# Gated cross-attention and quantised feed-forward: the mask becomes the bias of seven exponentials, scores move to PSUM, and the attention loop is put in another order

## The reference

```python
def _L0_xattn_ref(q, kv_src, seg_id, Wq, Wkv, Wo):
    qh = _split_heads(q @ Wq.T)
    k, v = jnp.split(kv_src @ Wkv.T, 2, axis=-1)
    gather = seg_id[:, :, None] - jnp.arange(4)
    neg_mask = gather < 0
    gc = jnp.clip(gather, 0, lkv - 1)
    k_sel, v_sel = kh[b_idx, :, gc], vh[b_idx, :, gc]       # transposed to b h q k d
    scores = jnp.einsum('bhqd,bhqkd->bhqk', qh, k_sel) * SCALE
    scores = jnp.where(neg_mask[:, None], neg_inf, scores)
    out = jnp.einsum('bhqk,bhqkd->bhqd', jax.nn.softmax(scores, axis=-1), v_sel)
    return out.transpose(0, 2, 1, 3).reshape(b, lq, D_ATTN) @ Wo.T

x = x + tanh(g_xattn[0]) * _L0_xattn_ref(layernorm(x), ctx, seg, Wq, Wkv, Wo)
x = x + tanh(g_ffn[0]) * _L0_ffn_ref(layernorm(x), W_in, b_in, W_out, b_out)
```

## Time and profile before

| | us |
|---|---|
| median of 3 runs | 355.43 (355.17 to 357.68) |
| the profiled execution | 353.4, its span 351.6 |
| busy: TensorE / VectorE / ScalarE / GpSimd | 289.5 / 316.8 / 207.7 / 171.8 |
| setup until the first product | 22.4 |
| attention loop (products of steps 1 to 16) | 22.4 to about 206.5 |
| last steps of attention and setup of the feed-forward part | to 225.4 |
| feed-forward part | 225.4 to 351.6 |

### The profile page before, as it was taken

The page is one execution under the profiler, slowest core; times in us unless marked ns, Lnnn a source line. Parts: engine busy times, 40 slices in busy tenths (PEclk is TensorE's granted clock), DMA queues, the critical chain, the costliest instruction groups (busy, mean ns, idle before and its releaser), DMA issues.

```text
span 351.6 us, 5786 instructions
## 1 busy us (share of the span) xinstructions
PE 289.5 (82%) x1807; PEld 210.5 (60%) x1807; DVE 316.8 (90%) x614; ACT 207.7 (59%) x323; POOL 171.8 (49%) x160
## 2 busy tenths in 40 slices
PE   3873779767679999999999955699799949999994
PEld 3442557555557777777777734344344418888883
DVE  0988599999998999999999999779999879999993
ACT  2132341251605666555556635899699969999991
POOL 1100638849497989889989882012243500110000
PEclk9998588885969999999999999699999998999999
DMA  7993000000000000000000000011112100435545
GB/s 259 282 389 111 0 0 0 2 1 0 2 2 0 0 2 0 3 0 2 1 2 1 3 0 0 0 62 60 60 61 102 77 1 2 62 60 76 98 64 119
DMA packets 6979, 17.26 MB, mean 49 GB/s; under 512 B 1318, under 2 KB 3822, under 8 KB 6446
## 3 DMA queue, kind: packets, MB, share of 16 engines
q1 hardware_dynamic: 4447, 12.31, 9.8%
q0 software_dynamic: 1008, 3.67, 6.8%
q10 hardware_dynamic: 1503, 1.02, 1.2%
HBM read 9.13 MB, written 7.86 MB: 48 GB/s over the span
## 4 chain that ended last, share of the span: by engine, by line
DVE 51%; PE 35%; issue 4%; ACT 4%; DMA 2%; POOL 2%; DVEq 0%; ACTq 0%; POOLq 0%
PE bank L786 16%; PE bank L756 12%; DVE prod L863 10%; DVE s L869 8%; DVE s L875 4%; PE bank L593 4%; DVE bn L820 3%; DVE xres L917 2%; DMA wq_ld<-in_L_xattn_Wq_dram 2%; PE bank L613 2%; DVE hmax L1117 2%; DVE onehot L969 2%; DVE xmax L923 2%; DVE s L884 2%; DVE bn L830 2%
## 5 line engine op out<-in xcount | busy, mean ns | idle before, releaser
L593 PE MATMUL bank<-kvtab,onehot 80*128 80x256 f16 x512 | 73.2, 291 | 26.3 <-DVE prod L863 17.1
L593 PEld LDWEIGHTS bank<-kvtab,onehot 80*128 80x128 bf16 x512 | 49.8, 103 | 46.1 <-DVE prod L863 22.4
L298 POOL TENSOR_TENSOR vsel<-vsel,pr 128x1024 f32<-128x1024 f32 x31 | 59.9, 1932 | 25.9 <-ACT vsel L348 20.3
L485 ACT ACTIVATE hidden<-bank,bin__58,zscale 128x512 f32 x64 | 49.6, 777 | 7.4 <-PE bank L756 2.2
L756 PE MATMUL bank<-xhi,win 128*128 128x512 f16 x128 | 49.3, 385 | 1.9 <-DVE xlo L1112 1.9
L756 PE MATMUL bank<-xlo,win 128*128 128x512 f16 x128 | 49.1, 384 | 0.0
L1177 DVE SCALAR_TENSOR_TENSOR hlo<-hq,rel_wout,hhi 128x512 f16<-128x512 int16 x64 | 46.0, 752 | 0.0
L863 DVE TENSOR_TENSOR prod<-bank,q 128x1024 f32<-128x1024 f32 x32 | 39.0, 1218 | 5.4 <-PE bank L593 5.3
L348 ACT ACTIVATE xT<-bank 128x512 f32<-128x512 f32 x16 | 9.5, 597 | 55.5 <-PE bank L644 55.5
L348 ACT ACTIVATE vsel<-bank 128x1024 f32<-128x1024 f32 x31 | 31.6, 1018 | 17.1 <-PE bank L593 17.1
L301 POOL TENSOR_TENSOR vsel<-vsel 128x512 f32<-128x512 f32 x31 | 40.4, 1302 | 2.4
(11 more groups left out here) (133 smaller groups left out, 479.8 us busy)
## 6 DMA issues: line engine op xcount, KB each, us to landing
xres<-in_x_dram SPq DMA_DIRECT2D x4, 1024.0 KB, 17.7
out_dram<-xres SPq DMA_DIRECT2D x7, 512.0 KB, 2.6
out_dram<-y POOLq DMA_DIRECT2D x7, 512.0 KB, 5.3
win_ld<-in_L_ffn_W_in_dram SPq DMA_DIRECT2D x1, 1024.0 KB, 12.4
wout_ld<-in_L_ffn_W_out_dram SPq DMA_DIRECT2D x1, 1024.0 KB, 23.1
seg_i<-in_itok_BxS_dram SPq DMA_DIRECT2D x3, 320.0 KB, 13.9
wkv_ld<-in_L_xattn_Wkv_dram SPq DMA_DIRECT2D x1, 512.0 KB, 4.9
seg_i<-in_itok_BxS_dram ACTq DMA_DIRECT2D x1, 320.0 KB, 9.2
```

Of the source, the lines that this page charges most:

```text
L298: pool.tensor_tensor(v3, v3, pr[k][:, t].rearrange("p o h -> p (o h)").unsqueeze(2).broadcast_to([P, KW * H, HD]), ALU.mult).then_inc(s_pv, 1)
L485: act.activation(hidden[:, g, f, :], bank, ACT.Gelu, bias=bin_[:, f:f + 1], scale=zscale[:, f:f + 1]).then_inc(s_h, 1)
L593: mm = pe.matmul(dst[:, off * D:(off + 1) * D], onehot[:, off, bass.ds(tile * P, P)], kvtab[:, b, part, col:col + D], start=(part == 0), s ...
```

## The change

Tables get three more rows in front (83 rows): an index below zero now gathers a copy of row 0, and its score is put out by a bias of -1e30 inside the exponential, a column of `neg` per tile and offset. So `mask` goes, and one exponential over 128 columns becomes seven: one of 32 columns for offset 0 of both tiles, six of 16 columns. Scores and exponentials share one place in PSUM, `sc`, in the first half of bank67, from which `ps_o` has moved out: the attention result's transpose now shares `ps_t` with the two other transposes.

The first norm of batches 1 to 3 moves from VectorE to ScalarE, in half batches of four tiles: sums, negative means, sums of squared differences. The clamps of batches 1 to 3 move to GpSimd, variance plus epsilon of the second norm from GpSimd to VectorE. `vsel` has four buffers instead of two. Lags change: v gathers and copies 1, residual 4, `norm_bias` 5, `norm2` 5, transpose of the second norm 6. The tables of batches 2 and 3 are scaled one at a time. W_out's maximum is taken after steps 13 and 14, its levels after step 15.

```diff
-                dve.tensor_tensor(s3, s3, neg[:, bass.ds(2 * u, 2), :]...broadcast_to([P, 2 * KW, H]), ALU.add).then_inc(s_masked, 1)
+        sc = [bank67[:, k * 2 * KW * H:(k + 1) * 2 * KW * H].rearrange("p (t o h) -> p t o h", t=2, o=KW) for k in range(2)]
...
             def exp(u, k):
                 act.wait_ge(s_shift, u + 1)
-                act.activation(e[k][:].rearrange(...), s[k][:].rearrange(...), ACT.Exp, scale=SCALE).then_inc(s_exp, 1)
+                act.activation(sc[k][:, :, 0, :], sc[k][:, :, 0, :], ACT.Exp, scale=SCALE)
+                for t in range(2):
+                    for off in range(1, KW):
+                        ins = act.activation(sc[k][:, t, off, :], sc[k][:, t, off, :], ACT.Exp,
+                                             bias=neg[:, 2 * u + t, off:off + 1], scale=SCALE)
+                ins.then_inc(s_exp, 1)
...
+            def stats1(b, half):
+                n = 2 * (b - 1) + half
+                act.wait_ge(s_x[b], 16)
+                if n:
+                    act.wait_ge(s_ssq1, n)
+                at = slice(b * TB + half * (TB // 2), b * TB + (half + 1) * (TB // 2))
+                for t in range(at.start, at.stop):
+                    ins = act.activation(unread[0][:, t % (TB // 2), :], xres[:, t, :], ACT.Copy, accum_out=sum1[:, t:t + 1])
+                ins.then_inc(s_sum1, 1)
+                act.wait_ge(s_sum1, n + 1)
+                act.activation(nmean1[:, at], sum1[:, at], ACT.Copy, scale=-1.0 / D).then_inc(s_nmean1, 1)
+                act.wait_ge(s_nmean1, n + 1)
+                for t in range(at.start, at.stop):
+                    ins = act.activation(unread[1][:, t % (TB // 2), :], xres[:, t, :], ACT.Square, bias=nmean1[:, t:t + 1],
+                                         accum_out=ssq1[:, t:t + 1])
+                ins.then_inc(s_ssq1, 1)
...
+            def clamp_seg(b):
+                pool.wait_ge(s_segb[b], 16)
+                pool.tensor_scalar(seg_b[:, b * LQ:(b + 1) * LQ]..., seg_i[:, b * LQ:(b + 1) * LQ]...,
+                                   float(TOP), 0.0, ALU.min, ALU.max).then_inc(s_segc, 1)
...
-            act.dma_start(ctx_ld[LKV:U, :, :], ctx_kv[:, LKV - 1, :].partition_broadcast(U - LKV)).then_inc(s_ctx, 16)
+            act.dma_start(ctx_ld[LB + LKV:U, :, :], ctx_kv[:, LKV - 1, :].partition_broadcast(LB)).then_inc(s_ctx, 16)
+            act.dma_start(ctx_ld[0:LB, :, :], ctx_kv[:, 0, :].partition_broadcast(LB)).then_inc(s_ctx, 16)
...
# TensorE's step
+                if on(0):
+                    transpose_x(i, k)
+                if on(1):
+                    gather_k(i - 1, 0)
+                    gather_v(i - 1, 0)
+                if on(6):
+                    transpose_xn2(i - 6, k, (s_xT, i + 1) if on(0) else (s_oT, i - 3))
+                if on(0):
+                    queries(i, k)
+                if on(1):
+                    gather_k(i - 1, 1)
+                if on(3):
+                    transpose_o(i - 3, 1 - k, (s_xn2T, i - 5) if on(6) else (s_xT, i + 1))
+                if on(1):
+                    gather_v(i - 1, 1)
+                if on(3):
+                    attn_out(i - 3, 1 - k)
...
# VectorE: behind aggregate, and the order of its first steps
+                dve.wait_ge(s_mv, u + 1)
+                dve.tensor_scalar(ve[k][:], mv[k][:, :, 1], LN_EPS, None, ALU.add).then_inc(s_ve, 1)
...
+            kv_scales(2, 1)
+            step(1, 1, between=lambda: kv_low(2))
+            kv_scales(3, 1)
+            step(2, 0, between=lambda: kv_low(3))
+            make_onehot(1)
...
+            for i in range(3, NP + 1):
+                step(i, i % 2)
+                if i in (6, 10):
+                    make_onehot(i // 3)
+                if i in (NP - 3, NP - 2):
+                    wout_amax(i - NP + 3)
+                if i == NP - 1:
+                    wout_levels()
...
# ScalarE's loop
-            for i in range(2, NP + 2):
+            for i in range(2, NP + 1):
                 step(i, i % 2)
+                if i in (2, 4, 5, 7, 8):
+                    stats1((i + 2) // 3, 0 if i in (4, 7) else 1)
```

More of the change, by code:

```diff
@@ L579, in transpose_o @@
                     pe.wait_ge(s_olast, 1)
-                if first(u, 1):
-                    pe.wait_ge(s_oT, u)
+                pe.wait_ge(*free)
                 for t in range(2):
                     for c in range(C):
-                        mm = pe.transpose(ps_o[:, c * 2 * P + t * P:c * 2 * P + (t + 1) * P], o[k][:, t, c * P:(c + 1) * P], ident[:])
+                        mm = pe.transpose(ps_t[:, c * 2 * P + t * P:c * 2 * P + (t + 1) * P], o[k][:, t, c * P:(c + 1) * P], ident[:])
                 mm.then_inc(s_oTp, 1)
@@ L626, in transpose_xn2 @@
                     pe.wait_ge(s_xn2b, 1)
-                if isinstance(u, int) and u + 5 > NP:
-                    pe.wait_ge(s_xn2T, u)
-                else:
-                    pe.wait_ge(s_xT, u + 5)
+                pe.wait_ge(*free)
                 for t in range(2):
@@ L637, in transpose_x @@
                 pe.wait_ge(s_x[u // (TB // 2)], 16)
-                if first(u, 5):
-                    pe.wait_ge(s_xn2T, u - 4)
+                if u >= 4:
+                    pe.wait_ge(s_oT, u - 3)
                 elif u:
@@ L697, in _ @@
             pe.wait_ge(s_kvlo, 2)
-            gather_k(0, 0)
+            step(1, 1)
+            pe.wait_ge(s_kvlo, 3)
             project_kv(3)
-            step(1, 1)
             def spread(psum, ready, done):
@@ L1019, in _ @@
             for off in range(KW):
-                ins = dve.tensor_scalar(neg[:, :, off], seg_f[:], float(off), NEG, ALU.is_lt, ALU.mult)
+                ins = dve.tensor_scalar(neg[:, :, off], seg_f[:], float(off), NEG_BIAS, ALU.is_lt, ALU.mult)
             ins.then_inc(s_neg, 1)
             dve.wait_ge(s_neg, 1)
-            step(1, 1)
-            kv_scales(2)
+            kv_scales(2, 1)
[3 more added lines that the diff above has]
+            make_onehot(1)
+            dve.wait_ge(s_tanh, 1)
             def top_of(psum, ready, out):
@@ new lines, in _ @@
+            for i in range(3, NP + 1):
[6 more added lines that the diff above has]
+                    wout_levels()
+            norm_bias(NP - 4, 0)
+            softmax_end(NP - 1, 1)
+            residual(NP - 3, 1)
+            stats2(NP - 3, 1)
+            aggregate(NP - 3, 1)
+            weigh_last(NP - 1, 1)
```

294 lines of the change are left out of this document (140 added, 154 removed).

## The result

The changed kernel takes **396.35 us** (median of 4 runs, 394.91 to 397.13); the kernel before, on the same chip, 355.36. The ratio is 1.113 [1.108, 1.119]: 41 us slower where 17 us faster was forecast, and far above the range. The profiled execution has a span of 394.9 us against 351.6.

The account below looks back on a forecast made before the run. VectorE was taken to set the pace, with TensorE and GpSimd 3.6 and 4.0 us behind over five steps. Terms of +3.6, -10.2, -12.9, +0.8 and +1.5 sum to -17.2, giving 338 us against the median; range 329 to 350.

Parts of the forecast that it names:

- the start: Up to step 1's first product: one more DMA issue, one table's scales and GpSimd's clamps add 3.6 us.
- steps 1 and 2: First two attention steps: W_out's maximum, broadcast and gather wait leave; 29.4 us becomes 19.2, so -10.2.
- steps 3 to 10: Attention loop: VectorE loses three batches of first-norm statistics and two clamps; 96.7 us becomes 83.8, so -12.9.
- steps 11 to 16: Late attention steps: six of 9.2 us plus 3.6 for W_out's maximum, against 58.0 us before, so +0.8.
- the tail: Between loop and feed-forward part: one more group of residual, statistics and norm, plus W_out's ratio, adds 1.5 us.
- The plain step of 9.2: Attention loop: three rings between 8.8 and 9.1 us hand on lateness, giving 9.2 us a step against 9.67.
- the ring by way of `xT`: Two-step chain through ScalarE's exponentials and xT copy, TensorE's queries to gather, and VectorE's step: 18.1 us, 9.05 a step.
- the share of a half batch that comes through: Steps 3 to 10: of ScalarE's 3.3 us half batch, 1.7 to 2.0 us lengthens each of four full steps.
- The clamps at the start: Three clamps on GpSimd land on the first one-hot and stretch VectorE's work: +2.5 us, ends 0 and +5.
- The rival in which GpSimd holds variance plus epsilon: VectorE's new small operation waits for GpSimd, 0.7 us on average in 12 steps: +8.4, 346 us; chance 0.20.
- The slower rival: ScalarE becomes the bound: exponentials at 0.59 us each, steps of 10.5 us, half batches 5.2: 364 us; chance 0.08.
- TensorE's low clock: Rival: TensorE stays at the lower clock through steps 3 to 6 and becomes the bound: +8, 346 us; chance 0.12.

Follow-up runs that it names:

- e1: The changed kernel with the index loads broadcast to 96 partitions instead of 83, the other 13 rows never read: 362.14 us.
- e10: The changed kernel with each of its four index loads issued as two, to 80 rows and to the last 3: 361.42 us.
- e5_xt_first: e1 with ScalarE's copy of the transposed x (xT) put ahead of the seven exponentials instead of behind them: 349.89 us.
- e9: e5_xt_first with GpSimd's three clamps held until VectorE has written the mask table `neg`: 350.87 us.
- e13: e9 with ScalarE's tanh of the gates moved behind its step 1: 343.95 us, ratio 0.967.
- e6: e5_xt_first with GpSimd's three clamps held until the one-hot rows of batch 0 are done: 350.72 us.
- e14: e5_xt_first (clamps beside the one-hot rows) with ScalarE's tanh of the gates moved behind its step 1: 349.88 us.
- e3: The kernel before with the mask part alone: 83 clipped rows (loaded to 96), no mask, seven exponentials, scores in SBUF, old order: 363.87 us.

## Why the prediction was wrong

**The step that failed is the start**, "+3.6", and with it steps 1 and 2, "-10.2". ScalarE's one more DMA issue was counted, but the four index loads that change from 80 to 83 rows were taken to be the same. They were not looked at as transfers: the term had no row for them, and its ends (0 to +5, for the port) left them out. The runs put about 34 us on them (e1 against the changed kernel), and e10 shows that it is their shape and not their bytes. No rival had it.

Without that fault the forecast would still have been 26 us short. By the terms, e1 lies above it by 5.6 at the start, 4.1 in steps 1 and 2, 10.6 in steps 3 to 10, 0.7 in steps 11 to 16 and 5.4 in the tail.

**Steps 3 to 10**, "-12.9", failed as well: without the load fault they gave -2.3. From one step's product to the next's, in us (the one-hots of batches 2 and 3 fall into steps 6 and 10):

| step | 3 | 4 | 5 | 6 | 7 | 8 | 9 | 10 |
|---|---|---|---|---|---|---|---|---|
| forecast | 8.0 | 9.0 | 10.9 | 13.3 | 9.2 | 10.9 | 10.9 | 11.6 |
| e1_rows96 | 12.3 | 8.1 | 12.3 | 16.9 | 8.8 | 9.7 | 12.9 | 13.6 |
| e5_xt_first | 9.0 | 8.4 | 10.3 | 13.2 | 8.8 | 8.9 | 10.1 | 13.2 |

The plain step of 9.2, and with it the ring by way of `xT` at 9.05, was about right: 8.8 in step 7, 8.8 and 9.7 in steps 11 and 12. What failed is the share of a half batch that comes through, 1.7 to 2.0 us "in each of four full steps", reckoned from ScalarE's idle time. In e1, against 9.2, steps 3, 5, 6 (without its one-hots) and 9 are longer by 3.0 to 4.1 us, which is nearly the whole half batch; only in step 8 is it hidden but for 0.5. ScalarE's queue has exponentials and xT behind the half batch, and TensorE stands until xT is copied and then runs at a lower clock for a while. e5 moves only that copy, the half batches stay, and steps 3, 5, 6 and 9 give 11.7 of its 12.6 us. The price of the ring also left out the transpose of the second norm, 0.46 us, which stands between xT's copy and the queries; no run separates it.

The half batches themselves were mis-sized too: 3.95 us (72.34 to 76.29) instead of 3.3, since each sum brings a second instruction of 0.19 us that reads the accumulator. And the two groups of one-hots in e1 took 3.56 and 4.22 us where 2.4 was taken for each, 3.0 of the 10.6.

```profile
L467 ACT ACTIVATION_READ_ACCUMULATOR unread<-xres 128x1 f32 x24 | 4.6, 192 | 0.0
L473 ACT ACTIVATION_READ_ACCUMULATOR unread<-xres,nmean 128x1 f32 x24 | 4.5, 186 | 0.0
```

**The clamps at the start** cost more than their upper end of +5, where +2.5 was taken. The one-hots took 7.01 us beside three clamps with 96 rows, +5.1; beside one clamp, as the loads left it in the changed kernel, 3.61. Held back behind `neg` (e5 to e9), they let the first product start 7.1 us sooner. The gates' load has its row (3.5 us of waiting before `tanhs`), but the forecast didn't name it.

**The tail**, "+1.5", is +6.1 to +6.9 in three kernels. One more group of residual, statistics and norm was priced, but not that the last attention output waits its turn behind it on ScalarE. Exchanging the two gave nothing. What in the longer chain costs isn't separated.

**Right**: VectorE's own step of 8.8 (8.78); the mask's 1.2 us; scores in PSUM at no cost; the exponentials at 1.3 or less (1.15); steps 11 to 16 in e13 within 0.6 us. The rival in which GpSimd holds variance plus epsilon, 0.7 us a step, came in a small part: that operation takes 0.32 us on average in e1, from 0.17 to 1.02. The slower rival's mechanism, exponentials of 0.59 us, did not occur. TensorE's low clock, given 0.12 as a rival of its own, came with its waits for xT (0.89 in e1, 17.0 us of them) and went as these were halved (0.98 in e5, 8.1 us). With the loads, the place of xT and the two delays of the start mended, e13 has the profiled sum of -13.5 us against -17.2 forecast; the tail alone is 4.6 over. That profile is of the fastest of its six runs; by the medians e13 gains 11.3.

## What to carry to other kernels

When a change alters the number of rows of a tile, follow each DMA that fills it: here four index loads to 80 rows had all landed by some 19 us, while with 83 rows the last of them was still awaited at 69 us, and both the queue that issues it and the loads behind it pay. A copy that lets another engine go on belongs ahead of longer work on its queue, even where that engine's busy share says it has time: here its place was worth 12 us. When an edit to a suspected delay gives nothing, look for a second one beside it before giving the first up: e6, e9 and e14 are all nil against e5, and e13 is 6 us.

## What the runs showed of the hardware

- Broadcast loads of 332 KB to 83 rows went at some 26 GB/s together, at a share of 0.06 of sixteen DMA engines, and two of them held their issuing queue 14.9 and 20.4 us. Of 320 KB to 80 rows, or 384 KB to 96, three took 1.5 us to issue in all, and the slowest landed 14.6 and 18.7 us after its issue, beside other loads.
- TensorE, idle for 2.27 us until 191.91, had a granted clock of 1.00 up to 193.0 us and then, though busy throughout, of 0.50 in 193.5 to 196.4.
- Four one-hots in bf16 on VectorE took 7.01 us beside three GpSimd clamps from int32 to bf16, and 1.91 alone. The small fp32 writes of `neg`, with one SBUF input, took 4.14 us beside them and 0.45 alone. The Trainium skill (SBUF — State Buffer, Who interferes with whom) has VectorE's two-port modes and GpSimd block each other for whole instructions; the runs agree.
- An activation with an accumulated output brings a second instruction of 0.19 us on ScalarE.
- Six exponentials of 128x16 with a bias per partition took 1.06 us in PSUM and 1.29 in SBUF (e3).
- Writes of VectorE into PSUM cost no more than into SBUF: the shift took 0.30 us in the changed kernel, against 0.29 in e3, where it lies in SBUF.
